# Attention scores paired in the two halves of the array's rows, and one rotation of two banks for a two-layer decoder block in fp32

## The reference, cut to what matters

```python
h  = layernorm(x)
q, k, v = h @ Wq, ctx @ Wk, ctx @ Wv            # 16 heads of 16, keys and values from ctx
s  = q @ k.T / 4                                # per head, 128 x 128
if layer == 1: s is masked (causal, and by the keys' mask)
o  = softmax(s) @ v
if layer == 0: o = o @ Wo + bo
x += tanh(g) * o
x += tanh(g2) * top2_experts(layernorm(x))      # 8 experts, each token goes to two
```

## Time and profile before

| | us |
|---|---|
| median of three runs | 1715.84 |
| lowest, highest | 1713.99, 1717.71 |
| the profiled execution | 1715.62 |
| its span in the trace | 1713.8 |
| TensorE, ScalarE, VectorE, GpSimd busy | 1595.4, 1233.1, 1199.4, 827.5 |

### The profile page before, as it was taken

One profiled execution on the slowest core, in us unless ns is written; L12 is line 12 of the kernel. 1 busy time (PEld: TensorE's weight loads), 2 busy tenths in 40 slices (PEclk: granted clock), 3 DMA queues, 4 the chain that ended last, 5 costly groups with the idle time before them and its releaser, 6 DMA issues.

```text
span 1713.8 us, 37210 instructions
## 1 busy us (share of the span) xinstructions
PE 1595.4 (93%) x12792; PEld 1406.1 (82%) x12792; DVE 1199.4 (70%) x2843; ACT 1233.1 (72%) x2859; POOL 827.5 (48%) x888
## 2 busy tenths in 40 slices
PE   6999999996899999999995999999994899999996
PEld 4777777774899999999994776776773899999996
DVE  4666777756577777777775778888866666666663
ACT  3887877771688888888872877777782577777774
POOL 3124433434365565656553113333323477777775
PEclk8999999996899999999997999999996999999998
DMA  3222222133877777788762223332231688887883
GB/s 108 50 51 74 72 73 75 51 87 87 246 237 229 227 231 226 229 227 232 225 191 72 76 82 104 98 95 72 90 92 65 204 236 227 225 241 222 229 230 98
DMA packets 208989, 256.57 MB, mean 150 GB/s; under 512 B 29555, under 2 KB 156788, under 8 KB 208800
## 3 DMA queue, kind: packets, MB, share of 16 engines
q1 hardware_dynamic: 186048, 218.22, 43.9%
q0 software_dynamic: 21120, 34.39, 7.8%
q10 hardware_dynamic: 1632, 1.58, 0.3%
HBM read 194.54 MB, written 45.74 MB: 140 GB/s over the span
## 4 chain that ended last, share of the span: by engine, by line
PE 76%; DVE 12%; issue 3%; POOL 3%; DMA 2%; ACT 2%; SPq 1%; POOLq 0%; DVEq 0%; ACTq 0%
PE ps L409 20%; PE ps L411 19%; PE ps L410 19%; PE ps L470 6%; PE ps L553 4%; PE ps L564 2%; DVE mx L1094 2%; POOL xs_scr L1345 1%; PE ps L534 1%; SPq L1444 1%; PE ps L495 1%; PE ps L488 1%; PE ps L526 1%; DVE X L1017 1%; PE ps L424 1%
## 5 line engine op out<-in xcount | busy, mean ns | idle before, releaser
L1217 POOL TENSOR_TENSOR KXR<-U,KXR 128x1024 fp32r<-128x1024 f32 (+1 forms) x156 | 355.4, 2278 | 278.4 <-ACT KXR L750 258.9
L409 PE MATMUL ps<-QR,KXR 128*128 128x256 f32 x1248 | 361.9, 290 | 4.2 <-DVE QR L1221 4.2
L411 PE MATMUL ps<-QR,KXR 128*128 128x256 f32 x1248 | 355.6, 285 | 0.0
L410 PE MATMUL ps<-QR,KXR 128*128 128x256 f32 x1248 | 355.4, 285 | 0.0
L750 ACT ACTIVATE KXR<-U 128x1024 fp32r<-128x1024 f32 (+1 forms) x312 | 287.4, 946 | 75.5 <-PE ps L411 50.4
L698 ACT ACTIVATE U<-ps,mx 128x128 f32<-128x128 f32 x1024 | 294.9, 391 | 26.3 <-DVE mx L1094 26.0
L409 PEld LDWEIGHTS ps<-QR,KXR 128*128 128x128 f32 x1248 | 241.8, 194 | 5.7 <-DVE QR L1221 5.3
L410 PEld LDWEIGHTS ps<-QR,KXR 128*128 128x128 f32 x1248 | 241.8, 194 | 0.0
L411 PEld LDWEIGHTS ps<-QR,KXR 128*128 128x128 f32 x1248 | 241.4, 193 | 0.0
L1094 DVE TENSOR_REDUCE mx<-ps 128x4 f32<-128x512 f32 x256 | 174.9, 685 | 87.2 <-PE ps L411 38.3
L1217 DVE TENSOR_TENSOR KXR<-U,KXR 128x1024 fp32r<-128x1024 f32 (+1 forms) x156 | 176.3, 1168 | 25.7 <-ACT KXR L750 25.5
(11 more groups left out here) (204 smaller groups left out, 4042.3 us busy)
## 6 DMA issues: line engine op xcount, KB each, us to landing
U<-in_wpack SPq DMA_DIRECT2D x234, 512.0 KB, 5.0
U<-in_wpack SPq DMA_DIRECT2D x78, 256.0 KB, 4.7
KXR<-U SPq DMA_DIRECT2D x512, 32.0 KB
U<-xs_scr SPq DMA_DIRECT2D x39, 258.0 KB, 4.5
U<-xs_scr SPq DMA_DIRECT2D x39, 257.0 KB, 4.7
U<-in_ctx_t SPq DMA_DIRECT2D x16, 512.0 KB, 5.4
U<-ys_scr SPq DMA_DIRECT2D x32, 256.0 KB, 3.3
XR<-in_L_ffn_b SPq DMA_DIRECT2D x39, 128.0 KB, 4.1
```

Of the source, the lines that this page charges most:

```text
L409: e.matmul(o, wh, xh, start=first, stop=False)
L410: e.matmul(o, wh, xl, start=False, stop=False)
L411: return e.matmul(o, wl, xh, start=False, stop=done)
L1217: e.tensor_tensor(w_cols(L, WL, n), w_raw(L, n), hi, ALU.subtract).then_inc(*l_w[n](L, i))
```

## The change

- **Scores in pairs.** `pe_scores` makes two units, i and i+1 with i even, in odd steps (i = s+3); even steps have no scores. Each matmul takes the 64 rows of its z only, for both operands, and the two units' matmuls alternate, each unit into its own bank. The pair waits for the exponentials of units i-3 and i-2 before its first matmul. Unit s+4 keeps its step; unit s+3 comes one step later than before.
- **Minima.** In even steps VectorE takes the minimum of the odd unit first, as before; in odd steps that of the even unit behind the divisions and the rests.
- **Banks.** Layer 0 rotates both banks, and the three uses that had `BO_` to themselves join the list: the bias of the output projection, the turned output, and its projection. Each waits for the use two before.
- **Steps.** The second key half is projected in step 1 of the period in place of 2, in both layers. The transposes of a batch's outputs stand behind the product with V of their step.

```diff
@@ -125,7 +125,7 @@
-X0, Q0, K0, V0 = (6, 7), (8, 9), (0, 2), (10, 11)
+X0, Q0, K0, V0 = (6, 7), (8, 9), (0, 1), (10, 11)
...
@@ -336,6 +336,12 @@
+                if L == 0 and s == 1:
+                    out.append((("bo", 0), s_bov[0]))
+                if L == 0 and (b := bat(s, 8)) is not None:
+                    out.append((("ot", b), v_ot[b]))
+                if L == 0 and (b := bat(s, 10)) is not None:
+                    out.append((("op", b), v_xup[0, b]))
...
         for L in LL:
-            uses, nb = uses_bk(L), L + 1
+            uses, nb = uses_bk(L), 2
...
@@ -442,6 +448,31 @@
+
+        def pe_scores(e, w, L, i):
+
+            b, m = i // 4, (i // 2) % 2
+            g, js, banks = b // G, slice(b % G * 128, b % G * 128 + 128), (SB_[i % 3], SB_[(i + 1) % 3])
+            w.wait_ge(*v_q[L, g, 1])
+            if i == 0:
+                for n in range(2):
+                    w.wait_ge(*a_v[L, 0, n])
+            w.wait_ge(*d_k[b % 2][L, b, 7])
+            for n in range(2):
+                if i + n >= 3:
+                    w.wait_ge(*a_p[L, i + n - 3])
+            for q, k in ((0, 0), (0, 1), (1, 0)):
+                for z, bank in enumerate(banks):
+                    hs = slice(64 * z, 64 * z + 64)
+                    ins = e.matmul(bank[:, :], QR[hs, g % 2, q, m, js], KX[hs, b % 2, k, m, 4 * z:4 * z + 4, :].rearrange("p h k -> p (h k)"),
+                                   start=(q, k) == (0, 0), stop=L == 0 and q == 1)
+                    if L == 0 and q == 1:
+                        ins.then_inc(*m_s(L, i + z))
+            if L == 1:
+                w.wait_ge(*v_mk[g])
+                w.wait_ge(*s_ir[0])
+                for z, bank in enumerate(banks):
+                    e.matmul(bank[:, :], IR[:, :], MK[:, g % 2, b % G:b % G + 1, :].to_broadcast([128, 4, 128]), start=False, stop=True).then_inc(*m_s(L, i + z))
 
         def pe_first(e, w, L):
 
@@ -469,31 +500,8 @@
                     for h in range(4):
                         ins = e.transpose(bank[:, h * 128:(h + 1) * 128], PB[:, i % 3, h], ident)
                     ins.then_inc(*m_t(L, i))
-                if 0 <= s + 4 < NU:
-                    i = s + 4
-                    b, m, z = i // 4, (i // 2) % 2, i % 2
-                    g, j, bank = b // G, b % G, SB_[i % 3]
-                    w.wait_ge(*v_q[L, g, 1])
-                    if i < 2:
-                        w.wait_ge(*a_v[L, 0, i])
-                    w.wait_ge(*d_k[b % 2][L, b, 7])
-                    if i >= 3:
-                        w.wait_ge(*a_p[L, i - 3])
-                    js = slice(j * 128, j * 128 + 128)
-                    kh, kl = (KX[:, b % 2, p, m, 4 * z:4 * z + 4, :].rearrange("p h k -> p (h k)") for p in range(2))
-                    ins = three(e, bank[:, :], (QR[:, g % 2, 0, m, js], QR[:, g % 2, 1, m, js]), (kh, kl), True, L == 0)
-                    if L == 1:
-                        w.wait_ge(*v_mk[g])
-                        w.wait_ge(*s_ir[0])
-                        ins = e.matmul(bank[:, :], IR[:, :], MK[:, g % 2, j:j + 1, :].to_broadcast([128, 4, 128]), start=False, stop=True)
-                    ins.then_inc(*m_s(L, i))
-                if (b := bat(s, 6)) is not None:
-                    bank = pt_place["o", b]
-                    w.wait_ge(*a_o[L, b])
-                    turn_free(w, L, "o", b)
-                    for n in range(4):
-                        ins = e.transpose(bank[:, n * 128:(n + 1) * 128], OS[:, n * 128:(n + 1) * 128], ident)
-                    ins.then_inc(*m_o(L, b))
+                if s % 2 and 0 <= s + 3 < NU:
+                    pe_scores(e, w, L, s + 3)
                 for name, at, project in (("xt", X0, pe_turn), ("q", Q0, pe_query), ("k", K0, pe_key), ("v", V0, pe_value)):
...
                 if L == 0 and s == 1:
                     w.wait_ge(*s_bo[0])
+                    bank_free(w, L, "bo", 0)
                     for t in range(2):
-                        ins = e.matmul(BO_[:, 0:D], ON[:, 0, t * 128:(t + 1) * 128], WS[:, 3, t], start=t == 0, stop=t == 1)
+                        ins = e.matmul(place[0, "bo", 0][:, 0:D], ON[:, 0, t * 128:(t + 1) * 128], WS[:, 3, t], start=t == 0, stop=t == 1)
                     ins.then_inc(*s_bomm(0))
                 if L == 0 and (b := bat(s, 8)) is not None:
                     w.wait_ge(*v_on[0, b])
-                    w.wait_ge(*(v_xup[0, b - 1] if b else s_bov[0]))
+                    bank_free(w, L, "ot", b)
                     for t in range(2):
-                        ins = e.transpose(BO_[:, t * 128:(t + 1) * 128], ON[:, b % 2, t * 128:(t + 1) * 128], ident)
+                        ins = e.transpose(place[0, "ot", b][:, t * 128:(t + 1) * 128], ON[:, b % 2, t * 128:(t + 1) * 128], ident)
                     ins.then_inc(*m_ot(b))
                 if L == 0 and (b := bat(s, 10)) is not None:
                     w.wait_ge(*v_ot[b])
                     w.wait_ge(*s_wl[0, 3])
+                    bank_free(w, L, "op", b)
                     for t in range(2):
-                        ins = three(e, BO_[:, 0:D], (OT[:, b % 2, 0, t, :], OT[:, b % 2, 1, t, :]), (WR[:, 3, 0, t], WR[:, 3, 1, t]), t == 0, t == 1)
+                        ins = three(e, place[0, "op", b][:, 0:D], (OT[:, b % 2, 0, t, :], OT[:, b % 2, 1, t, :]), (WR[:, 3, 0, t], WR[:, 3, 1, t]), t == 0, t == 1)
                     ins.then_inc(*m_op(b))
                 for p in PARTS:
                     k = (L,) + p.key
@@ -553,6 +563,13 @@
...
                     ins.then_inc(*m_av(L, i))
+                if (b := bat(s, 6)) is not None:
+                    bank = pt_place["o", b]
+                    w.wait_ge(*a_o[L, b])
+                    turn_free(w, L, "o", b)
+                    for n in range(4):
+                        ins = e.transpose(bank[:, n * 128:(n + 1) * 128], OS[:, n * 128:(n + 1) * 128], ident)
+                    ins.then_inc(*m_o(L, b))
...
@@ -1083,15 +1100,17 @@
 
+        def dve_least(e, w, L, i):
+            w.wait_ge(*m_s[L, i])
+            if i >= 4:
+                w.wait_ge(*a_p[L, i - 4])
+            e.tensor_reduce(mx[:, i % 4], SB_[i % 3][:, :].rearrange("p (h k) -> p h k", h=4), AX.X, ALU.min).then_inc(*v_mx(L, i))
+
         def dve_attention(e, w, L):
             dve_first(e, w, L)
             for s in range(FIRST, LAST):
-                if 0 <= s + 3 < NU:
-                    i = s + 3
-                    w.wait_ge(*m_s[L, i])
-                    if i >= 4:
-                        w.wait_ge(*a_p[L, i - 4])
-                    e.tensor_reduce(mx[:, i % 4], SB_[i % 3][:, :].rearrange("p (h k) -> p h k", h=4), AX.X, ALU.min).then_inc(*v_mx(L, i))
+                if s % 2 == 0 and 0 <= s + 3 < NU:
+                    dve_least(e, w, L, s + 3)
                 if (b := bat(s, 7)) is not None:
                     w.wait_ge(*m_o[L, b])
                     o = pt_place["o", b][:, :].rearrange("p (h d) -> p h d", d=32)
```

More of the change, by code:

```diff
@@ L715, in act_attention @@
                         w.wait_ge(*m_op[b - 2])
-                    e.activation(OT[:, b % 2, 0].rearrange("p t n -> p (t n)"), BO_[:, 0:256], ACT.Copy).then_inc(*a_ot(b))
+                    e.activation(OT[:, b % 2, 0].rearrange("p t n -> p (t n)"), place[0, "ot", b][:, 0:256], ACT.Copy).then_inc(*a_ot(b))
                 for p in PARTS:
@@ L890, in dve_rests @@
                 oh, ol = (OT[:, b % 2, z].rearrange("p t n -> p (t n)") for z in range(2))
-                e.tensor_tensor(ol, BO_[:, 0:256], oh.bitcast(F32), ALU.subtract).then_inc(*v_ot(b))
+                e.tensor_tensor(ol, place[0, "ot", b][:, 0:256], oh.bitcast(F32), ALU.subtract).then_inc(*v_ot(b))
             if L == 0 and (b := bat(s, 10)) is not None:
@@ L894, in dve_rests @@
                 w.wait_ge(*p_xb[b])
-                e.scalar_tensor_tensor(X[:, b], BO_[:, 0:256], th[:, 0:1], X[:, b], ALU.mult, ALU.add).then_inc(*v_xup(0, b))
+                e.scalar_tensor_tensor(X[:, b], place[0, "op", b][:, 0:256], th[:, 0:1], X[:, b], ALU.mult, ALU.add).then_inc(*v_xup(0, b))
             for p in PARTS:
@@ L1127, in dve_attention @@
                     w.wait_ge(*s_bomm[0])
-                    e.tensor_tensor(bo[:, :], bo[:, :], BO_[:, 0:D], ALU.add).then_inc(*v_c.up())
+                    e.tensor_tensor(bo[:, :], bo[:, :], place[0, "bo", 0][:, 0:D], ALU.add).then_inc(*v_c.up())
                     w.wait_ge(*v_c.now)
```

## The result

The changed kernel takes 1748.93 us (median of 4 runs, 1747.34 to 1754.2), the kernel before 1715.93 beside it: ratio 1.0198, 95% interval 1.0173 to 1.0223. Forecast were 1685 us and a gain; it is 33 us slower and outside the range. The profiled execution is the slowest of the four, 1754.2 us (span 1752.4).

The account below looks back on a forecast made before the run. TensorE was taken to bound layer 0 and the second part of layer 1's period, VectorE the first part; savings of 21 us in layer 0 and 9 in layer 1 off 1715.6 gave 1685, range 1645 to 1716.

Parts of the forecast that it names:

- part 1: Score pairs on TensorE: row halves run side by side, saving 0.48 us a pair in layer 0, 0.40 in layer 1.
- Part 4: Steps 3 and 4 in layer 0: ScalarE can't keep up with TensorE's bare double step, costing 0.9 us a period.
- hidden: Turned outputs behind the product with V: moves 0.44 us within a step, at no cost, since VectorE reads a step later.
- Part 2: Layer 0's bank rotation and earlier key half: shortens the rank matmul's wait, saving 0.55 us a period (0 to 0.98).
- Part 3: First query projection, step 8: without even-step scores TensorE waits 0.7 us a period, both layers (0.3 to 1.0).
- nothing is gained: Layer 1's first 28 us of a period: VectorE bounds it and loses no work, so the gain there is zero.
- A: Score pair on TensorE: the halves take turns, costing 1.40 us plus switches; 26 us slower, 1742; chance 14%.
- B: Score pairs and partner engines: the switch is free and the partners follow; 1650 us or a little under; chance 12%.
- C: Two-step ring of scores, minimum, exponential and next pair: up to 0.41 us lost per pair; about 1716; chance 10%.
- a wait of TensorE before scores: Sign for C: TensorE idle before a score matmul released by an exponential, in every double step.

Follow-up runs that it names:

- e2: The kernel before with only the rotation of both banks in layer 0 and the second key half in step 1; 1705.02 us, ratio 0.9953.
- e16: The changed kernel with pairs only in steps 5 and 13 of both layers, single 128-row units elsewhere; 1701.25 us, ratio 0.9915.
- e10: The changed kernel with pairs only in the double steps ending in steps 1 to 7, single 128-row units elsewhere; ratio 1.0162.
- e3: The changed kernel's schedule with each score matmul over all 128 rows again; 1774.67 us, ratio 1.0361.
- e15: The changed kernel with a pair only in step 13 of both layers, single 128-row units elsewhere; ratio 0.9929.
- e11: The changed kernel with pairs only in steps 11, 13 and 15 of both layers, single 128-row units elsewhere; ratio 0.9947.
- e9: The changed kernel with pairs only in the double steps ending in steps 9 to 15, single 128-row units elsewhere; ratio 0.9999.
- e4: The changed kernel with twelve idle-filling matmuls ahead of each group's first turn of x; 1745.49 us, ratio 1.0184.
- e5 to e8: The changed kernel with projections moved into emptied steps, the norm in VectorE's step 4, or combinations, some with output transposes first; ratios 1.0094, 1.0087, 1.0113, 1.0102.

## Why the prediction was wrong

**The step that failed is the sum of part 1**: eight pairs a period on TensorE's path, because TensorE bounds the period. It did, with no margin: in e2 TensorE is busy for all of a period, and still the turn of x stands right behind VectorE's run of routing. A pair taken out of steps 2 to 5 (e16) gives nothing, four early ones cost 4.3 a period in layer 0 (e10 against e2), 3.0 of it at a clock of 1.00 (its second period, 47.12 against 44.08). I read VectorE's 32 busy us of 45 as slack; where its work comes in one piece there is none, and I had seen that in layer 1 alone.

**Part 4 named the place and the wrong partner.** It charged 0.9 a period for ScalarE in steps 3 and 4. TensorE waits for no exponential there in layer 0; it waits 3.10 for VectorE at step 6. The charge should have been worked out as the time from VectorE's last free moment to its norm, against TensorE's bare steps.

**Part 1, the sizes.** The pair alone is right: 0.89, against 0.85 for 0.70 and a switch in front, and e3's 1.39 without overlap. The switches were taken too low: 0.22 for both in layer 0, a full one in front and half of one behind, where the one behind alone measured 0.20 if a projection follows. The new place of the turned outputs, "hidden", costs about 0.15: from start to start the four transposes, with what they change in those behind them, add 0.43 or 0.59 us behind the product with V, by turns, against 0.35 behind scores. All in all, one pair saves 0.34 (e15), three 0.26 each (e11), eight (44.08 - 41.93)/8 = 0.27, where 0.48 had been taken. With 0.27 for each pair in both layers and nothing else changed, layer 0 would have come to 2.2 + 0.55 - 0.7 - 0.9 = 1.15 a period, layer 1 to 1.1 - 0.35 = 0.75, and the forecast to 1715.6 - 7.5 x 1.9 = 1701: still a gain.

The estimate from the Trainium skill (TensorE: Matmul & The Clock Gate, Part 3) put the pair's matmuls at 0.91, without a switch. Measured are 0.89 with a part of the switches in it, and the 0.24 from the second two starts to the third is the price of one matmul: the overlap was fuller than that estimate. The Trainium skill (TensorEngine Tiling (Array Packing), Key Properties) has a change of the tiling mode drain the engine; the trace here has 0.20 more behind a pair, and does not show what takes them.

**Part 2** was right in direction: 0.55 forecast, 1.12 measured (e2), above its upper end of 0.98. The wait went to nothing there; in the changed kernel it stays at 0.88 (0.4 forecast). I had taken 2.09 us from the key half's last matmul to the rank matmul; they became 2.93 (127.61 to 130.54), because VectorE comes to the key half only behind its routing and a minimum. The key half's instruction on VectorE, after:
```profile
129.66 0.74 DVE L894 SCALAR_TENSOR_TENSOR U<-ps,bqk,U 128x512 fp32r<-128x512 f32 x1
```
So this term too had VectorE's run wrong.

**Part 3** was right: 0.7 forecast (0.3 to 1.0), 0.56 measured, and e9 against e11 shows it alone in layer 0. That the clock falls in every other period of e9 as well was not foreseen.

**Layer 1**: "nothing is gained" in VectorE's 28 us, but I let it be neutral. It lost 4.3 us a period, and 20 of the 33 us are lost there: 3.6 of idle time and 2.8 of clock, less 2.1 of saved work.

**The clock** is in no term of the sum. Behind a wait of 3.1 us it stands at 0.60 on the mean (layer 0), behind one of 2.6 at 0.51 (layer 1), at or near its 1.2 GHz level, for some 4 to 6 us. The books price that at 1.5 and 2.8 us a period, and the periods of e4 at the same. With four such periods in each layer this is an estimate of 17 of the 33 us, if nothing else had taken their place; e4 got back 3.

**Rivals.** A is excluded by the chain and by e3. B is excluded by the 0.20. C came nearest: it said that the pair's hand-over makes the bare double step stiff, but placed it at the score pair, with idle time released by an exponential. That wait is 0.6 a period in layer 1, and there is none in layer 0. The rival that was missing is VectorE's run at steps 3 to 5, with the turn of x behind it. What was named as a sign, a wait of TensorE before scores, would have missed it.

## What to carry to other kernels

Before a saving on the busiest engine is counted, ask for each step where it lies what its engine waits for next: in front of a hand-over from a partner that is busy without a gap, it turns into waiting. Here pairs gained in steps 11, 13 and 15 of layer 0 and lost in steps 1 to 7; whether other work, put into the emptied steps, saves the early ones is not shown (e5 to e8). Test one pair before eight. And measure the harmless-looking part of a change alone: here the rotation of banks, with one projection moved by a step, was a gain of 8 us that the pairs buried.

## What was not expected of the hardware

- Two row halves of 64 rows, six fp32 matmuls of 512 columns into two banks, take 0.89 us, against 1.39 for six over 128 rows; the first matmul of a projection behind them takes 0.43 in place of 0.23.
- With a wait of 0.56 us a period the granted clock fell in every other period of e9's layer 0 (0.96 and 45.2 us against 1.00 and 43.7). The kernel before waits 0.98 us there and kept 1.00 in every period, and in e10's layer 1, with a wait of 2.6 us, most periods kept 1.00. So the length of the wait alone does not tell whether the clock falls.
- The same kernel before took 1713 to 1716 us beside most runs and 1756 and 1759 beside two groups of them. In the traces of these groups ScalarE and VectorE stood still for up to 5.6 us at a time with a releaser that the trace calls remote. The cause is open. Ratios from the two settings should not be set beside each other.
